# A decoder layer on one core: the attention probabilities are transposed by VectorE and two DMA trips instead of TensorE

## The reference

```python
x = _rmsnorm(hidden_states, ln_weight)
h_q = (x @ w_q.T).reshape(b, lq, H, DH)
h_k = (key_value_states @ w_k.T).reshape(b, lk, H, DH)
h_v = (key_value_states @ w_v.T).reshape(b, lk, H, DH)
score = jnp.einsum('bqhd,bkhd->bhqk', h_q, h_k)
score = score + position_bias[None]
m = attention_mask[:, None]
score = jnp.where(m, score, -jnp.inf)
score = jax.nn.softmax(score, axis=-1)
score = jnp.where(m, score, 0.0)
attn = jnp.einsum('bhqk,bkhd->bqhd', score, h_v).reshape(b, lq, H * DH)
out = attn @ w_out.T
return hidden_states + out
```

## Time and profile before

| | |
|---|---|
| median of three runs | 911.64 us (909.94 to 913.21) |
| the profiled execution: its own time, its span | 913.16 us, 911.3 us |
| TensorE busy | 904.1 us of the span, granted clock 0.996 |
| VectorE, ScalarE, GpSimd busy | 699.7 us, 516.7 us, 667.0 us |
| scores L736, first and last start | 389.8 us and 864.6 us |
| TensorE's part of the chain that ended last | 87% |

### The profile page before, as it was taken

How to read it: one execution, slowest core, us unless ns; L and a number is a source line. 1 busy time by engine, 2 the same in 40 slices (tenths; PEclk the granted TensorE clock), 3 DMA queues, 4 the chain that set the end, 5 groups by cost and what they waited for, 6 DMA issues and landing times.

```text
span 911.3 us, 15431 instructions
## 1 busy us (share of the span) xinstructions
PE 904.1 (99%) x5150; PEld 778.2 (85%) x5150; DVE 699.7 (77%) x761; ACT 516.7 (57%) x1190; POOL 667.0 (73%) x431
## 2 busy tenths in 40 slices
PE   9999999999999999999999999999999999999998
PEld 7687688888888888788899999999899999999876
DVE  5789997999999999556666667676767676767784
ACT  3686858576565575365655555555555555555330
POOL 3246779897758778367698878888988878787522
PEclk9899999999999999999999999999999999999999
DMA  9545566666686754357645454545444445454302
GB/s 310 162 139 175 158 198 194 203 202 196 189 273 198 247 160 169 122 170 228 194 137 158 136 158 135 158 137 160 136 159 135 160 134 168 132 168 137 104 1 93
DMA packets 96850, 150.26 MB, mean 165 GB/s; under 512 B 10577, under 2 KB 35281, under 8 KB 96673
## 3 DMA queue, kind: packets, MB, share of 16 engines
q1 hardware_dynamic: 86432, 131.54, 44.2%
q10 hardware_dynamic: 10368, 18.09, 7.9%
HBM read 113.81 MB, written 35.78 MB: 164 GB/s over the span
## 4 chain that ended last, share of the span: by engine, by line
PE 87%; DVE 10%; issue 1%; DMA 1%; ACT 1%; POOL 0%; DVEq 0%; ACTq 0%; SPq 0%
PE acc L509 11%; PE acc L511 11%; PE acc L510 11%; PE misc L511 6%; PE misc L509 6%; PE misc L510 6%; PE acc L736 6%; PE acc L791 6%; PE acc L668 5%; PE acc L669 5%; PE acc L670 5%; DVE misc L1232 4%; PE acc L760 3%; DVE w L1239 2%; DVE misc L1227 2%
## 5 line engine op out<-in xcount | busy, mean ns | idle before, releaser
L1494 POOL TENSOR_TENSOR y<-y,w 128x2048 f32<-128x2048 f32 x31 | 143.5, 4629 | 58.3 <-DVE w L1239 57.3
L1232 DVE TENSOR_TENSOR_SCAN misc<-dA,misc 128x2048 f32<-128x2048 f32 x32 | 141.7, 4429 | 4.2 <-ACT dA L863 1.0
L1084 ACT ACTIVATE prob<-prob,negm 128x128 f32<-128x128 f32 x256 | 99.9, 391 | 43.7 <-DVE negm L1302 43.7
L1091 ACT ACTIVATE ot_hi<-acc 128x512 fp32r<-128x512 f32 x64 | 38.3, 598 | 143.0 <-PE acc L791 143.0
L1555 POOL TENSOR_TENSOR wt_lo<-ws,wt_hi 128x1024 fp32r<-128x1024 f32 x27 | 65.0, 2408 | 61.0 <-ACT wt_hi L1072 58.9
L509 PE MATMUL misc<-wo_hi,ot_hi 128*128 128x512 f32 x256 | 107.1, 418 | 0.0
L511 PE MATMUL misc<-wo_hi,ot_lo 128*128 128x512 f32 x256 | 101.3, 396 | 0.0
L509 PE MATMUL acc<-wv_hi,ctx_hi 128*128 128x512 f32 x256 | 101.0, 395 | 0.0
L510 PE MATMUL misc<-wo_lo,ot_hi 128*128 128x512 f32 x256 | 100.8, 394 | 0.0
L1572 POOL TENSOR_TENSOR wo_lo<-wo_raw,wo_hi 128x512 fp32r<-128x512 f32 x64 | 95.7, 1495 | 6.2 <-ACT wo_hi L1048 6.2
L510 PE MATMUL acc<-wv_lo,ctx_hi 128*128 128x512 f32 x256 | 99.9, 390 | 0.0
(11 more groups left out here) (198 smaller groups left out, 2448.9 us busy)
## 6 DMA issues: line engine op xcount, KB each, us to landing
k_scratch<-kst SPq DMA_DIRECT2D x64, 256.0 KB, 3.5
bc<-xp_scratch ACTq DMA_DIRECT2D x32, 512.0 KB, 5.8
v_scratch<-vst SPq DMA_DIRECT2D x32, 512.0 KB, 4.0
k_sb<-k_scratch SPq DMA_DIRECT2D x64, 256.0 KB, 2.7
v_sb<-v_scratch SPq DMA_DIRECT2D x64, 256.0 KB, 2.6
wo_raw<-in_wo SPq DMA_DIRECT2D x64, 256.0 KB, 2.9
wp<-in_wq SPq DMA_DIRECT2D x54, 256.0 KB, 3.7
wraw<-in_wk SPq DMA_DIRECT2D x32, 256.0 KB, 5.1
```

What stands on the lines that cost most here:

```text
L1084: last = act.activation(prob[q][:, b], prob[q][:, b], ACT.Exp, bias=negm[q][:, b:b + 1], accum_out=psum[q][:, b:b + 1])
L1232: dve.tensor_tensor_scan(h_ps, flat(dA[k % 2][:, :, :, :]), h_ps, 0.0, ALU.mult, ALU.add).then_inc(da_free, 1)
L1494: pool.tensor_tensor(y_half(half), y_half(half), w[:, k % 2], ALU.add).then_inc(y_ready, 1)
```

## The change

VectorE has an instruction that transposes every 32x32 block of a tile in its place. The change uses it on the normalized probabilities (function `turn`, STREAM_TRANSPOSE into the new tile `blocks`), which leaves the sixteen blocks of a 128x128 transpose right inside and in the wrong places. A transfer writes `blocks` to a scratch in DRAM (`p_scratch`, 256 KB), and four transfers of 64 KB each read it back into `pt_sb`, one for each group of 32 partitions, in pieces of 512 bytes. TensorE's transposes and VectorE's copy of their result are gone. The product with the values comes a step later (`pv(g - 3)` instead of g-2) and stands ahead of the output projection, which is now that of head g-4. High and low parts of output and of output weights move a step later with them. SyncE loads values and output weights a step later, waits for `turned`, issues the write, and in the next step waits for its landing (`blocks_out`), ahead of the loads of keys and bias. Two of the Strassen products change places in even steps. A few parameter loads move from steps 4 to 6 to around step 32, `o_sum` shares the place of `ea_sb`, four more steps are written out behind step 35, and there is one more step at the end.

```diff
+    p_dram = nc.dram_tensor("p_scratch", (2, 4, 32, 4, HT // 4), F32, kind="Internal").ap()
...
-        pt_sb = [sb(whole, f"pt_sb{i}", [P, HB, S]) for i in pair]
+        pt_sb = [sb(whole, f"pt_sb{i}", [P, 4, HB, 32]) for i in pair]
...
+        blocks = [sb(whole, f"blocks{i}", [P, 4, HB, 32]) for i in pair]
+        o_sum = ea_sb
...
@@ SyncE, step
+                if runs(g - 2):
+                    sp.wait_ge(blocks_out[p], in_count(g - 2, p, 16))
+                    for k in range(4):
+                        sp.dma_start(pt_sb[p][32 * k:32 * (k + 1), :, :, :].rearrange("j q b i -> j q (b i)"),
+                                     p_dram[p, :, :, k].rearrange("q j x -> j q x")).then_inc(pt_in[p], 16)
                 if runs(g) and runs(g + 1):
                     if not known(g) or g >= 1:
                         sp.wait_ge(sb_done, g)
                     load_kb(g + 1, head(g + 1, half), 1 - p)
-                if runs(g):
-                    if not known(g) or g >= 2:
-                        sp.wait_ge(pv_done, g - 1)
-                    sp.dma_start(v_sb[p][:, :, :].rearrange("p b d -> p (b d)"), v_dram[g]).then_inc(v_in[p], 16)
...
+                if runs(g - 1):
+                    if not known(g) or g >= 3:
+                        sp.wait_ge(pv_done, g - 2)
+                    sp.dma_start(v_sb[1 - p][:, :, :].rearrange("p b d -> p (b d)"), v_dram[g - 1]).then_inc(v_in[1 - p], 16)
+                    if not known(g) or g >= 3:
+                        sp.wait_ge(wo_lo_done, g - 2)
+                    sp.dma_start(wo_raw[1 - p][:], a["wo"][(g - 1) % H if known(g) else g - 1 - H * half]).then_inc(wo_in[1 - p], 16)
+                    sp.wait_ge(turned, g)
+                    sp.dma_start(p_dram[1 - p].rearrange("q j k x -> (q j) k x"),
+                                 blocks[1 - p][:, :, :, :].rearrange("p k b i -> p k (b i)")).then_inc(blocks_out[1 - p], 16)
...
@@ TensorE, step
-                if runs(g - 2):
-                    pe.wait_ge(p_ready, g - 1)
...
-                        pe.wait_ge(ot_lo_done, g - 2)
-                    for b in range(HB):
-                        mm = pe.transpose(psT[:, b * S:(b + 1) * S], prob[p][:, b], ident[:])
-                    mm.then_inc(t_done, 1)
...
                 if runs(g - 3):
...
+                    pv(g - 3, 1 - p)
+                if runs(g - 4):
+                    h = (g - 4) % H if known(g) else 1
...
+            def pv(h, p):
+
+                pe.wait_ge(pt_in[p], in_count(h, p, 64))
+                pe.wait_ge(v_in[p], in_count(h, p, 16))
+                if known(h) and h == 0:
+                    pe.wait_ge(sum_evac, slot(NG, 0) - 1)
+                else:
+                    pe.wait_ge(ot_lo_done, h)
+                for b in range(HB):
+                    mm = pe.matmul(psO[:, b * S:(b + 1) * S].rearrange("p (q i) -> p q i", q=4), v_sb[p][:, b],
+                                   pt_sb[p][:, :, b], start=True, stop=True)
+                mm.then_inc(pv_done, 1)
...
@@ VectorE, step
-                if runs(g - 2):
-                    dve.wait_ge(t_done, g - 1)
-                    if not known(g) or g > 3:
-                        dve.wait_ge(pv_done, g - 3)
-                    dve.tensor_copy(pt_sb[p][:, :, :].rearrange("p b q -> p (b q)"), psT).then_inc(pt_evac, 1)
...
                     dve.tensor_tensor(q_sb[0][:, HALF_T:HT], sumX, q_u[:], ALU.add).then_inc(c12_done, 1)
+                    turn(g - 1, q)
...
+            def turn(h, q):
+
+                dve.wait_ge(p_ready, h + 1)
+                if not known(h) or h >= 2:
+                    dve.wait_ge(blocks_out[q], in_count(h - 2, q, 16))
+                dve.transpose(blocks[q][:, :, :, :].rearrange("p k b i -> p b k i"),
+                              prob[q][:, :, :].rearrange("p b (k j) -> p b k j", j=32)).then_inc(turned, 1)
```

More of the change, by code:

```diff
@@ L296, in decoder_layer @@
         mx_done, exp_done, rec_done = sem("mx_done"), sem("exp_done"), sem("rec_done")
-        p_ready, t_done, pt_evac, pv_done = sem("p_ready"), sem("t_done"), sem("pt_evac"), sem("pv_done")
+        p_ready, turned, pv_done = sem("p_ready"), sem("turned"), sem("pv_done")
+        blocks_out, pt_in = [sem(f"blocks_out{i}") for i in pair], [sem(f"pt_in{i}") for i in pair]
         ot_hi_done, ot_lo_done, o_done, x2_done = sem("ot_hi_done"), sem("ot_lo_done"), sem("o_done"), sem("x2_done")
@@ L329, in pipeline @@
                     step(4 * i + p, p, 0, 2 * i + p // 2)
-            for g in range(H - 4, H + 4):
+            for g in range(H - 4, H + 8):
                 step(g, g, g // H, g // 2)
                 behind(g)
-            with eng.Fori(H // 4 + 1, STEPS // 4 - 1) as i:
+            with eng.Fori(H // 4 + 2, STEPS // 4 - 1) as i:
                 for p in range(4):
                     step(4 * i + p, p, 1, 2 * i + p // 2)
-            for g in range(STEPS - 4, STEPS + 3):
+            for g in range(STEPS - 4, STEPS + 4):
                 step(g, g, 1, g // 2)
@@ L712, in step @@
                 elif paired(i) and not p:
+                    pe.wait_ge(s1_done, count(i))
+                    product(sumX, W12, pp, *z_of(half, 1, 0), False).then_inc(p2_done, 1)
                     pe.wait_ge(wc_lo, count(i))
@@ L777, in step @@
                     mm.then_inc(o_done, 1)
+                if known(g) and g == STEPS + 2:
+                    f_input(0, (weff_sum, C), (sb_done, STEPS), (c21_done, count(PAIRS - 1)), (ot_lo_done, STEPS))
                 if paired(i) and not p:
@@ L1086, in step @@
                     last.then_inc(exp_done, 1)
-                if runs(g - 2):
-                    act.wait_ge(pv_done, g - 1)
-                    if not known(g) or g > 3:
-                        act.wait_ge(o_done, g - 3)
-                    act.activation(ot_hi[p][:], psO, ACT.Copy).then_inc(ot_hi_done, 1)
+                if runs(g - 3):
+                    act.wait_ge(pv_done, g - 2)
+                    if not known(g) or g > 4:
+                        act.wait_ge(o_done, g - 4)
+                    act.activation(ot_hi[1 - p][:], psO, ACT.Copy).then_inc(ot_hi_done, 1)
                 if known(g) and g == STEPS:
@@ L1327, in step @@
                                       ALU.mult).then_inc(p_ready, 1)
+                    if not paired(i):
+                        turn(g - 1, q)
                 if paired(i) and not p:
@@ L1605, in step_and_tail @@
                     inverse_root(5, 0)
-                if known(g) and g == H + 1:
-                    pool.wait_ge(ffn_in, 16 * 6)
+                if known(g) and g == STEPS - 3:
+                    pool.wait_ge(ffn_in, 16 * 9)
                     for e in range(ER):
```

71 lines of the change are left out of this document (29 added, 42 removed).

## The result

The change made the kernel slower: 981.74 us in the median of three executions (978.73 to 982.23) against 910.79 us before (four executions), a ratio of 1.077 (1.0745 to 1.0788), 71 us. A fourth execution took 2259.61 us and is left out; nothing here shows why. The forecast was 893.6 us and a gain. What happened is rival (d), SyncE's ring, at a larger size than the 936 us it was given.

A forecast was written before the change was run, and what follows sets the result against it. TensorE, busy for 904.1 of 911.3 us, was taken as the bound. The terms -27.5 + 3 + 5 + 1.5 = -18 us took the median of 911.64 to 893.6 us; forecast 888 to 898, range 887 to 914.

The forecast's parts named there:

- rival (d): SyncE's queue binds: at a landing of 3.5 us, 7.8 us a step, 936 us in all, slower; chance 0.10.
- The landing of the write: Time for the 256 KB write of `blocks` from SBUF to DRAM: 2.0 to 2.5 us.
- the ring: SyncE's loop of write, landing and eight issues: 6.3 to 6.8 us against 7.1, hidden while a landing stays under 2.8.
- Issues: Eight issues behind the landing in SyncE's queue, 0.53 us apart: 4.2 us.
- Volume: DMA engines get 512 KB more per step on about 1.1 MB; their share goes from 0.49 to about 0.75.
- Transposes removed: TensorE's queue loses 64 groups of four transposes, 0.43 us each: -27.5 us.
- The block transpose: New VectorE instruction behind the normalization, priced like the row maximum: 0.69 us.
- rival (c): VectorE's transpose and GpSimd hold each other off: 1.44 us in place of 0.69, 926 us, slower; chance 0.11.
- VectorE's chain: Scores' add to next query piece, with the transpose: 13.9 us a pair of steps against TensorE's 14.2; VectorE just keeps up.
- The moved steps: Product with values and projection come a step later; TensorE waits in steps 2 and 3: 3 us lost, bounds 0 and 3.6.
- (b): Rival: VectorE is the bound by a little, a pair of 14.3 us or more: 898 to 909; chance 0.18.
- VectorE's odd jobs, uneven steps: VectorE's one-time work no longer hidden, 5 us lost, bounds 0 and 6; 1.5 more for the normalization's varying length.

The follow-up runs named there:

- e3: The change as made, but no read waits for its step's write and no product for the reads, block ordering left out: 899.09 us.
- e1: The change as made, with the write of the blocks issued ahead of the loads of values and output weights: 904.03 us, ratio 0.9928 to before.
- e8: The change as made, with loads of values and output weights bringing only 32 of 128 partitions from step 4 on: 901.02 us, ratio 0.9895.
- e4: The change as made, with one more 16-byte transfer per step in SyncE's queue: 1018.34 us, 37 us more than the change.
- e5: e2 with the last query piece of each step issued in the middle of the projection: 888.04 us, ratio 0.975 to before.
- e2: The change as made without both DMA trips; the product with the values reads the block tile directly, blocks unordered: 898.77 us, ratio 0.9863.

## Why the prediction was wrong

**The landing of the write (the step that failed).** "I take 2.0 to 2.5, because the queue waits for VectorE before each write and has then drained." It took 4.6. The sentence made an outcome into its own reason. The queue drains only while SyncE is early; the ring was given 6.3 to 6.8 us against a step of 7.1, a slack of 0.3 to 0.8 us. Behind keys, bias, values and weights (0.81 MB) the landing is over the 2.8 us at which the slack ends even where nothing waits for it in the queue, 3.0 us in e3. In the change as made it is 2.2 us once, 2.9 and 3.7 in the next two steps, and with all four loads issued in the 2 us ahead of the write, 4.6. The priced 2.0 to 2.5 do come true in e1 (2.1), where the write stands ahead of values and weights: the figure belonged to another place in the queue. I had the decisive figures in hand, the limit of 2.8 and the 3.5 us of the earlier trace rows, and gave (d) one chance in ten. The rival's size was off for the same reason: it took a fixed landing of 3.5 us for a quantity that grows with the ring's lateness. The Trainium skill (DMA: Bandwidth & Descriptors, Queues, rings and completion order) says that each DMA engine consumes the descriptors of a ring in order; the runs agree, with 2.1 us behind keys and bias alone (0.31 MB, e1), 2.2 behind 0.44 MB (e8), and 3.0 (e3) and 4.6 (the change as made) behind 0.81 MB.

**Issues.** 8 x 0.53 = 4.2 us were priced, 3.91 measured (write to write, less the landing). e4 confirms the price of one, 0.57 us. The time of the ring is then 8.55 us a step. The maximum's first and last starts lie 539.1 us apart (L1315, 391.5 to 930.6), 8.56 a step, where it was 7.52 (L1302 in the earlier trace rows).

**Volume.** Priced at nothing but a share of about 0.75 for the DMA engines; right: 0.3 us (e3), with a share of 0.81 in 520 to 640 us.

**Transposes removed.** -27.5 us, 0.43 a step: right. e5's maxima run from 390.0 to 837.0, 447.0 us where the earlier trace rows have 474.0.

**The block transpose.** 0.69 us priced, 0.701 measured, with no mutual hold with GpSimd: right, and rival (c) is out. VectorE's chain of 13.9 us against 14.2 was near enough: e5 runs pairs of 14.12. Its wait for the high part did go, as foreseen: 53.1 us in 60 steps before, 2.7 us once in e5.

**The moved steps.** 3 us lost: right within what can be told. e2 and e5 wait 3.2 us for `ot_lo` once, at the start of the attention, and from the last maximum to the end it is 48.8 us in e5 (885.8 - 837.0), 45.6 before. But I looked only at what the move delays, not at what the moved product had covered: up to 0.37 us a pair at the start of the scores, and 10.7 us in all between e2 and e5. The sum had no term for it. The sign was in the text (TensorE waiting for pieces of the query product in every pair), under (b) and with VectorE's speed as the reason; the reason was a place in TensorE's order.

**VectorE's odd jobs, uneven steps.** 5 + 1.5 us: too dear. e5 comes out at 888.0 beside 911.3 for the kernel before in its round; 911.3 - 27.5 + 3 is 886.8, which leaves 1.2 for both. So the sum's -18 came within 5.4 us of e2 by luck: two terms overpriced by some 5 us stand beside a missing one of 10.7.

## What to carry to other kernels

When a change puts a wait for a landing into the queue that also issues the loads, write the queue's loop as a sum (landing plus issues) and take the landing with everything that stands ahead of it in the queue. Here a queue that was once late issued its loads in one burst and stayed late. Put the transfer that somebody waits for ahead of the loads that nobody waits for yet: here that alone was worth 78 us. When an instruction is moved, ask at its old place what latency it covered.

## What was not expected of the hardware

- The 256 KB write from SBUF to DRAM landed in 2.1 us ahead of the loads of values and weights, with the DMA engines busy to 0.80 (e1, 520 to 640 us), and in 4.6 us behind 0.81 MB on the same queue, with the engines busy to 0.67 only. Their share of busy time didn't tell how long the transfer took; its place in the queue did.
- STREAM_TRANSPOSE of 128x512 float32 took 699 to 712 ns in 64 cases beside a GpSimd that was busy to 69% of the span; it was as steady as the one-input maximum (685 to 690 ns in the same run).
- A transfer of 16 bytes cost the queue 0.57 us a step (e4), as much as a larger one: 0.46 to 0.57 us lie between the issues of keys, bias, values and weights in the timeline of the change as made.
